# Taking 36 gather steps per edge phase off GpSimd's queue and fetching their rows by one DMA per edge from SyncE

## What is computed

```python
h     = relu(layernorm(x))
w     = edge_weight / max(wsum, 1e-12)[dst]
feat  = relu(h @ W_pool + b_pool)
neigh = segment_max(feat[src] * w, dst)            # 0 where deg is 0
rst   = h @ W1_self + neigh @ W1_neigh + b1
h1    = relu(rst / norm(rst))
neigh2 = segment_sum(h1[src] * w, dst) / max(deg, 1)
out   = x + relu(h1 @ W2_self + neigh2 @ W2_neigh + b2)
```

## Time and profile before

| | us |
|---|---|
| median of 3 runs | 4948.29 (4942.51 to 4954.36) |
| span of the profiled execution | 4111.7 |
| median less the span: what lies around it | 836.6 |

### The profile page before, as it was taken

How to read it: one execution, slowest core, us unless ns; L and a number is a source line. 1 busy time by engine, 2 the same in 40 slices (tenths; PEclk the granted TensorE clock), 3 DMA queues, 4 the chain that set the end, 5 groups by cost and what they waited for, 6 DMA issues and landing times. The chain is left out here.

```text
span 4111.7 us, 30816 instructions
## 1 busy us (share of the span) xinstructions
PE 2558.4 (62%) x7403; PEld 1175.2 (29%) x7403; DVE 2819.4 (69%) x6223; ACT 1349.0 (33%) x3994; POOL 3076.6 (75%) x3262
## 2 busy tenths in 40 slices
PE   4133342222377787874667777777776777779956
PEld 3033232222122332321422222222322222224534
DVE  6477787877567776775567677767776777776524
ACT  5334443333333333332532233222232233223420
POOL 7777777777777777776767777777777777777766
PEclk8555555555699999997589989999899999899755
DMA  7233334444433333333433433433433433433445
GB/s 203 87 110 109 105 120 125 125 128 130 128 104 118 107 113 111 104 111 102 102 94 107 113 107 107 117 106 104 116 106 107 114 106 110 113 104 104 114 110 149
DMA packets 393546, 468.02 MB, mean 114 GB/s; under 512 B 57650, under 2 KB 323252, under 8 KB 380948
## 3 DMA queue, kind: packets, MB, share of 16 engines
q0 software_dynamic: 104000, 213.25, 19.8%
q1 hardware_dynamic: 289364, 252.80, 19.1%
HBM read 240.76 MB, written 225.06 MB: 113 GB/s over the span
## 5 line engine op out<-in xcount | busy, mean ns | idle before, releaser
L445 POOL DMA_INDIRECT G<-h_tab,SRC x1511 | 1425.7, 944 | 471.8 <-issue 411.7
L445 POOL DMA_INDIRECT G<-feat_tab,SRC x1451 | 1375.8, 948 | 442.2 <-issue 394.4
L767 DVE TENSOR_SCALAR CP<-pH,kc 128x512 f32<-128x512 f32 x1862 | 1387.2, 745 | 44.0 <-PE pM L923 43.2
L544 ACT ACTIVATE pT<-G,EW 128x128 f32<-128x128 f32 x1522 | 552.8, 369 | 1175.7 <-DMA G<-h_tab,SRC 594.4
L544 ACT ACTIVATE pM<-G,EW 128x128 f32<-128x128 f32 x1440 | 510.4, 367 | 1265.5 <-DMA G<-feat_tab,SRC 599.9
L923 PE MATMUL pM<-CP,A 128*128 128x512 f32 x1372 | 722.8, 679 | 204.4 <-DVE CP L767 204.3
L923 PE MATMUL pC<-CP,A 128*128 128x512 f32 x1176 | 589.1, 646 | 217.9 <-DVE CP L767 217.8
L899 PE MATMUL pH<-CP 128*128 128x98 bf16 x1563 | 144.8, 282 | 603.7 <-DVE CP L725 603.7
L710 DVE SCALAR_TENSOR_TENSOR S<-S,C,pT 128x128 f32<-128x128 f32 x782 | 269.6, 345 | 339.6 <-ACT pT L544 326.6
L713 DVE SCALAR_TENSOR_TENSOR S<-S,M,pT 128x128 f32<-128x128 f32 x782 | 266.9, 341 | 320.9 <-ACT pT L544 313.6
L923 PEld LDWEIGHTS pM<-CP,A 128*128 128x128 f32 x1372 | 260.0, 212 | 653.0 <-DVE CP L767 488.4
(11 more groups left out here) (134 smaller groups left out, 1804.8 us busy)
## 6 DMA issues: line engine op xcount, KB each, us to landing
scan<-S SPq DMA_DIRECT2D x97, 1032.0 KB
scan<-S SPq DMA_DIRECT2D x97, 1024.0 KB
G<-h_tab,SRC POOLq DMA_INDIRECT x1511
G<-feat_tab,SRC POOLq DMA_INDIRECT x1451
feat_tab<-F SPq DMA_DIRECT2D x24, 256.0 KB, 2.5
h_tab<-A SPq DMA_DIRECT2D x24, 256.0 KB, 2.6
U<-in_x SPq DMA_DIRECT2D x24, 256.0 KB, 3.8
out<-F SPq DMA_DIRECT2D x24, 256.0 KB, 2.5
```

What stands on the lines that cost most here:

```text
L445: pool.indirect_dma_start(out=dst, out_offset=None, in_=table, in_offset=bass.IndirectOffsetOnAxis(ap=idx, axis=0)).then_inc(s, 16)
L544: act.activation(scaled(t), v, ACT.Copy, scale=EW[:, t:t + 1]).then_inc(s_mul, 1)
L767: dve.tensor_scalar(OH[:, k % 4, :], pH[:, :], kc[:, j:j + 1], None, ALU.is_equal).then_inc(s_o2, 1)
```

## The change

SyncE fetches the rows of 36 steps per phase. The steps lie one in every two or three blocks, at place 9 of a block (`ROWT`). A step's 128 rows are eight chunks of 16 (`RL`); in each turn of `store_blocks` but the last one or two SyncE fetches three chunks (`RC`) ahead of its wait for the block's end. For a chunk it reads 16 byte addresses from the new tile `IX` into registers with one load and issues 16 DMAs, each of one row of 512 bytes, whose source address is in a register, into one partition of one of two new slots `GR`. The last chunk of a step is fetched in the block before the one that uses the step. ScalarE waits for all 128 DMAs of the step. The 72 steps leave `GORD`, and with it GpSimd's queue. `NX` falls from 32 to 16. One more load at the start brings `IX`, and one instruction of VectorE turns row numbers into byte addresses.

```diff
-NX = 32
+NX = 16
...
+RC = 3
+RL = 16
+CH = P // RL
+NGS = 2
+ROWT = [T * ((CH * k + CH - 1) // RC + 1) + 9 for k in range((RC * (NB - 1)) // CH)]
+NROW = len(ROWT)
+RAT = {(phase, t): phase * NROW + k for phase in range(2) for k, t in enumerate(ROWT)}
+ROWORD = list(RAT)
+GORD = [(0, t) for t in SEQ if (0, t) not in PAT and (0, t) not in RAT] + \
+    [(1, t) for t in range(TS) if (1, t) not in PAT and (1, t) not in RAT]
...
+                    sp.dma_start(IX[:, :], srcr).then_inc(s_ixl, 16)
...
+            regs = [sp.alloc_register(f"row{i}") for i in range(RL)]
+            flat = [tab.rearrange("n d -> (n d)").bitcast(U8) for tab in (feat, htab)]
+
+            def fetch_rows(phase, c):
+
+                k, i = phase * NROW + c // CH, c % CH
+                if c == 0:
+                    if phase == 0:
+                        sp.wait_ge(s_ix, 1)
+                        all_done(sp, s_fst, NGR)
+                    else:
+                        all_done(sp, s_hst, NGR)
+                if i == 0 and k >= NGS:
+                    ph, before = ROWORD[k - NGS]
+                    sp.wait_ge(s_mul, ph * TS + before + 1)
+                sp.load(regs, IX[k:k + 1, i * RL:(i + 1) * RL])
+                for r in range(RL):
+                    p = i * RL + r
+                    at = sp.snap(regs[r])
+                    sp.dma_start(GR[p:p + 1, k % NGS, :].bitcast(U8),
+                                 flat[phase][bass.ds(at, 4 * D)].rearrange("(a d) -> a d", a=1))\
+                        .then_inc(s_row[k % NGS], 16)
...
+                    for c in range(RC * b, min(RC * (b + 1), CH * NROW)):
+                        fetch_rows(phase, c)
                     sp.wait_ge(s_cmb, phase * TS + r[-1] + 1)
...
+                elif (phase, t) in RAT:
+                    k = RAT[phase, t]
+                    act.wait_ge(s_row[k % NGS], 16 * P * (k // NGS + 1))
+                    v = GR[:, k % NGS, :]
...
+                    dve.wait_ge(s_ixl, 16)
+                    dve.tensor_scalar(IX[:, :], IX[:, :], 9, None, ALU.logical_shift_left).then_inc(s_ix, 1)
```

More of the change, by code:

```diff
@@ L52 @@
 PAT = {(QUADS[u][0], t): (u, i) for u in range(QN) for i, t in enumerate(quad_steps(u))}
-GORD = [(0, t) for t in SEQ if (0, t) not in PAT] + [(1, t) for t in range(TS) if (1, t) not in PAT]
+RC = 3
[6 more added lines that the diff above has]
+ROWORD = list(RAT)
+assert all(t < TS and t not in XAT and (phase, t) not in PAT for phase, t in RAT)
+GORD = [(0, t) for t in SEQ if (0, t) not in PAT and (0, t) not in RAT] + \
+    [(1, t) for t in range(TS) if (1, t) not in PAT and (1, t) not in RAT]
 LT = 8
@@ L77 @@
 I32 = mybir.dt.int32
+U8 = mybir.dt.uint8
 def tiles_of(g):
@@ L107, with build @@
 OWN = own_rows()
-def build(nc, x, src, srcq, dstx, ew, w_pool, b_pool, w1s, w1n, b1, w2s, w2n, b2, out):
+def build(nc, x, src, srcq, srcr, dstx, ew, w_pool, b_pool, w1s, w1n, b1, w2s, w2n, b2, out):
     feat = nc.dram_tensor("feat_tab", (NP, D), F32).ap()
@@ L127, in build @@
         G = sb("G", [P, NG, D])
+        GR = sb("GR", [P, NGS, D])
+        IX = sb("IX", [P, P], I32)
         S = sb("S", [P, NS, T, RW])
@@ L239, in build @@
         s_xg = [sem(f"s_xg{i}") for i in range(NX)]
+        s_row = [sem(f"s_row{i}") for i in range(NGS)]
+        s_ixl = sem("s_ixl")
+        s_ix = sem("s_ix")
         s_mul = sem("s_mul")
@@ L1000, in _ @@
             node_stage(1, s_y)
-_NAMES = ["x", "src", "srcq", "dstx", "ew", "w_pool", "b_pool", "w1s", "w1n", "b1", "w2s", "w2n", "b2"]
+_NAMES = ["x", "src", "srcq", "srcr", "dstx", "ew", "w_pool", "b_pool", "w1s", "w1n", "b1", "w2s", "w2n", "b2"]
 def kernel(x, src, dst, edge_attr_128, edge_weight, L0_gnn_W_pool, L0_gnn_b_pool, L0_gnn_W1_self,
@@ L1022 @@
     srcq = np.stack([srcs[:, list(quad_steps(u))].T.reshape(-1) for u in range(QN)])
-    given = [filled(x, 0, NP, 0), srcs[:, order], srcq, dstx, filled(edge_weight, 0, EP, 0),
+    srcr = filled(np.stack([srcs[:, t] for _, t in ROWORD]), 0, P, 0)
+    given = [filled(x, 0, NP, 0), srcs[:, order], srcq, srcr, dstx, filled(edge_weight, 0, EP, 0),
              L0_gnn_W_pool, L0_gnn_b_pool, L0_gnn_W1_self, L0_gnn_W1_neigh, L0_gnn_b1,
```

## The result

| | us |
|---|---|
| kernel before, 4 runs | 4946.49 (4942.51 to 4954.36) |
| changed kernel, 4 runs | 7905.76 (7903.77 to 7916.56) |
| ratio | 1.599, 95% interval 1.596 to 1.602 |
| span of the profiled execution, after | 7914.8 |

The kernel became slower by 2959 us. The direction was forecast; the size was not: 5192 us, and a range from 4960 to 5700. In the experiments the kernel before takes 4113 us on three chips and 4945 on two. By these times its profile ahead of the prediction (span 4111.7) is of the first kind, and its runs and those of the changed kernel are of the second. So nothing "lies around the span".

A forecast was written before the change was run, and what follows sets the result against it. GpSimd's gathers were taken to bound both edge phases at 1.248 us each. Removing 72 wins 90 us, SyncE's longer turns lose 334, so 4948 + 244 = 5192 us; the forecast's own range was 4960 to 5700.

The forecast's parts named there:

- lies around the span: Runs of 4948 us against a span of 4111.7: difference left unchanged; growth with instructions, +250 us, given little weight.
- What bounds the kernel before: Both edge phases run at GpSimd's pace, 1.248 us per gather; 72 gathers fewer are worth 90 us.
- Where the loss comes from: SyncE's turn in `store_blocks` outgrows GpSimd's block and sets its length: 334 us lost; this forecast's chance 0.44.
- the signs named: No SyncE wait at block's end, blocks of 19 to 21 us, gathers waiting for ScalarE, VectorE waiting for the store.
- By which path: VectorE waits for the store's landing, three blocks on; rows come 11 us before use, at no cost.
- One-row DMA plus copy: In SyncE's turn, 0.322 us a row; the DMA alone 0.272, so 48 DMAs take 13.1 us.
- the 2.4 us that stand in the sum for 48 copies: In SyncE's turn, the term for 48 register copies and addresses in registers: 2.4 us.
- The load: In SyncE's turn, loading 16 registers from SBUF: 1.1 us each, 3.3 for three, between 0.15 and 5.4.
- The hold behind the store in phase 1: The first row DMA of every phase 1 turn is held behind the block's store: +1.5 us.
- The sum: SyncE's turn: 13.1 + 2.4 + 3.3 + 0.6 = 19.4 us in phase 0, 20.9 in phase 1.
- the prediction's own last step: Turns set against GpSimd's blocks: 106 + 26 + 202 = 334 us lost, 90 won, +244.
- rival (2): SyncE far over its block: turns of 26.7 and 28.2 us, about 6590 us; above 5700, chance 0.16.

The follow-up runs named there:

- e14_rc1: Changed kernel with one chunk of 16 rows per turn in place of three: 4083.11 us beside 4113.44 for the kernel before, ratio 0.9927.
- e15_static: Changed kernel with the row DMAs' addresses fixed in the program, without register loads and copies: 4024.11 us, where the kernel before takes 4113.
- e8_after: The changed kernel itself, unaltered, run again on the first kind of chip: 5351.81 us beside 4113.01 for the kernel before.
- e3_nogather: Changed kernel with only the first 16 gathers of the edge phases: 5473.63 us beside 4945.69 for the kernel before.
- e12_16rows: Changed kernel with gathers of 16 rows in place of 128 after the first 16: 8233.68 us beside 4945.09 for the kernel before.
- e13_poolwork: e3_nogather with GpSimd filling a scratch tile in place of each gather left out: 5477.86 us beside 4945.09 for the kernel before.

## Why the prediction was wrong

Point by point, by its own steps.

- **What bounds the kernel before**: right on chips of the first kind, where 24 gathers fewer were worth 30 us (e14_rc1) and 72 were worth 89 (e15_static). On the others the kernel before takes 832 us more, and it has waits that the profile at hand didn't have (VectorE idles 1222.6 us at L767 in place of 44.0).
- **Where the loss comes from**: right. SyncE's turn no longer fits into a block and sets its length; the signs named came: almost no wait at the block's end, gathers behind ScalarE. On the first kind of chip blocks 20 to 52 are as long as the others (25.7 and 25.3 us in e8_after).
- **By which path**: wrong. It was to be the landing of the stores, on which VectorE waits, while the rows were to be there 11 us before their use at no cost. In e8_after VectorE waits 30 us for stores and ScalarE 2170 for rows (848 and 2681 us in the changed kernel on the other kind): with SyncE behind, the rows are late first. The length of a block is SyncE's turn either way.
- **One-row DMA plus copy**: 0.322 us a row taken, 0.387 measured in the median. The trace has two copies per DMA (9216 at L408, as many at L407), where one was assumed; they cost 0.056 and 0.067 with their gaps, close to the 0.05 taken for one. No run shows the 2.4 us that stand in the sum for 48 copies: two per row are 48 x 0.123 = 5.9 us. They do add up, as none of SyncE's 28688 instructions in e8_after starts before the one ahead of it has ended. With the slower ones among them the 48 rows are 19.2 us, not 15.5.
- **The load**: 1.1 us each taken. Measured on the first kind of chip: 1.25 in the median for the second and third of a turn, and 2.6 to 4.2 for the first, which stands behind the store: 5.7 us a turn in phase 0 and 5.9 in phase 1, for 3.3. No run shows the 1.1 us, which was the author's estimate, or that a load takes 1.8 us at the most (5.4 for three): the shortest load of e8_after takes 1.16 us, the longest 4.23. That SyncE waits for a load is measured: in e8_after each of the 576 loads is followed by its first copy, 0.02 to 0.35 us after its end.
- **The hold behind the store in phase 1**, +1.5 us: right where a row DMA stands directly behind the store (e15_static, 17.0 us for the rows against 15.6). In the changed kernel it did not come on top: turns are 25.5 us in phase 0 and 25.8 in phase 1, since a load now stands ahead of the first row. It is this load that is long (2.6 to 4.2 us, where the others take 1.25); that it is held by the store itself is likely but not tested.
- **The sum**: 25.5 and 25.8 us a turn in place of 19.4 and 20.9. Put into the prediction's own last step, they give 20 x 6.0 + 33 x 9.3 + 43 x 6.7 + 96 x 7.0 - 90 = 1297 us. Measured on the first kind of chip: 5352 - 4113 = 1239. So the structure held and its terms were too small: the turn lay in what was given as rival (2), with 26.7 as the end of its bounds. Each unknown was priced too near to its lower end, and the second copy was not foreseen.
- **The step that failed outright**: "the difference from the median of the runs" was put down to something around the span and left alone. It was 837 us inside the kernel. The span and the time of one execution differ by 1.8 us (7914.8 and 7916.56). A profile that is 17% quicker than every run shown does not describe the runs, and no row of it could give the 2554 us between the two kinds of chip, of which SyncE's slowed instructions make some 2430: 7906 us there, 5352 on the others. That 5352 lies inside the forecast range is luck: the range stood on a base of 4948 us, and on a base of 4113 the prediction's own gain and loss give 4357.

What stays open: why a gather slows SyncE's instructions by 0.7 us or twice that on some chips, or at some times, and not on others. That the slowing needs the gathers is shown (e3_nogather), and that it goes neither by their rows (e12_16rows) nor with GpSimd's being busy (e13_poolwork). e3_nogather and e13_poolwork also show that VectorE's waits in the changed kernel need the gathers (60.2 and 58.2 us in place of 1065.3). For the kernel before, the same was not tried on a chip of the second kind.

## What to carry to other kernels

Before a queue takes on per-element work, write its turn out instruction by instruction (here two copies and a DMA per row, a load per 16) and set it against the shortest block, not the mean one; a small dose (16 rows per turn) may win a little where the full one loses. Where the span of the profile is not the time of the runs, settle that before anything is summed from it. And price an engine's many small instructions on a kernel that runs the other queues as well: SyncE idle on the page was no sign that it had room.

## What was not expected of the hardware

- On two of the five chips that the experiments ran on, many instructions of SyncE, copies of registers among them, stand 0.70 or 1.40 us apart where GpSimd issues gathers, in total about as many as there are gathers, with 128 rows each or 16. VectorE gets waits in the same steps, and both are gone without the gathers. The kernel before takes 4113 us on three of the chips and 4945 on these two.
- A load of 16 registers from one row of SBUF: 1.25 us in the median, and 2.6 to 4.2 right behind the issue of a store of 1 MB (e8_after).
- A one-row DMA: 0.23 us of SyncE, 0.26 to the start of the register copy that follows it (e8_after); 0.295 from start to start when the next such DMA follows (e15_static). Right behind a store, the first few such DMAs are held: 1.72, 1.09 and 0.81 us behind one of 2048 pieces.
